# Four-layer graph network on one core: h of the last layer transposed by VectorE instead of TensorE, dot products and spreading of the scores moved

## The chip, the cores and the metric

The kernel runs on one core of one Trainium2 chip. The metric is the device time in microseconds (us) of one execution; lower is better. Three executions of the kernel before took 2621.48, 2621.51 and 2623.4 us (median 2621.51). Engines are named PE (TensorE matmuls), PEld (TensorE weight loads), DVE (VectorE), ACT (ScalarE), POOL (GpSimd) and SP (SyncE, which here only issues DMAs).

## The reference

64 graphs, each with x of 256 nodes by 512 features and an adjacency matrix adj of 256 by 256, all fp32. Four layers, each behind a layer norm and a relu, each added to x:

```
h = relu(layernorm(x));  x = x + layer(h)
layer 0: Wh = h W; e = leaky_relu(Wh a1 + (Wh a2)^T, 0.2), masked by adj > 0.5
         att = softmax(e, axis=1);  out = elu(att Wh)
layer 1: A1 = D^-1/2 (adj + I) D^-1/2;  out = relu(A1 h K + bias)
layer 2: out = relu((adj h) K), rows of h that are all zero masked
layer 3: out = relu([h, adj h / deg] W^T)
```

The output is x after the fourth layer, fp32. To keep fp32 accuracy, every matmul is done as three matmuls on a high and a low part of its operands (hi hi, hi lo, lo hi), in the fp32r type.

## The kernel before

**Staging.** Each pair (graph, layer) is a step k = 4 graph + 5 layer. So the layer of a step is k mod 4, and the steps of a layer follow each other at a distance of four. All engines run the same loop over slots j; in slot j each engine does its part of steps j-1 to j+5, so that five graphs are under way at once. A period is four slots and finishes one graph. Below, "slot 0" is every slot with j mod 4 = 0, and so on: in slot 0, step j is of layer 0, j+1 of layer 1, j+2 of layer 2, j+3 of layer 3. The order within a slot is written out by hand, engine by engine, and semaphores with counted values join the engines. An engine executes strictly in its order.

**A step of layers 0 to 2.** DVE takes the statistics of x (`statistics`, L540 to L545), POOL works out scale and bias (`normalise`, L730 to L741), ACT writes h (`activate`, L405) and its high part h_hi (`high_part`, L411), POOL the low part h_lo (`low_part`, L747). PE multiplies h by the adjacency matrix or the attention (`gather`, 24 matmuls of 256 columns) into the PSUM tile T; ACT and DVE split T into t_hi (`gathered`, L417) and t_lo (L595), in two halves each; PE multiplies by the weights (`project`, 24 matmuls of 512 columns) into O; in the next slot ACT, DVE and POOL apply the nonlinearity and add to x.

**Layer 3** has the order of products turned round, and needs h transposed. PE's `transpose_h` (L302 to L311) makes eight transposes of 128x128 blocks of h into the PSUM tile X; ACT copies them to ht_hi (L423), DVE makes ht_lo (L602). Then `project_first` (24 matmuls of 512 columns into T), `gathered`, and in `gather_last` 24 matmuls of 512 columns into X and 12 into O.

**Attention scores of layer 0.** `dots` (L554, DVE, four operations of 128x512) forms the products of h with two vectors; PE's `spread` (L298) transposes the result so that it lies along rows of X; DVE's `mask_scores` (L569 to L576), ACT's `exps` (L453, L457) and DVE's `softmax_parts` (L581 to L589) make the attention's parts p_hi and p_lo, which `gather` of layer 0 waits for.

**Order per slot in the kernel before** (what the step is of, in brackets):

- PE: slot 0 `gather`[1], `project`[0]; slot 1 `gather`[2], `transpose_h`[3], `project`[1]; slot 2 `spread`[0], `project_first`[3], `project`[2]; slot 3 `gather`[0], `gather_last`[3].
- DVE: slot 0 `mean_relu`[3] (L627, L630), `gathered`[1], `with_self` (L649 to L654, the adjacency with its diagonal for a later layer 1), `dots`[0]; slot 1 `positive_part`[0] (L608), `gathered`[2], `add_mask` (L562), `transposed`[3] (L602), `statistics`[1]; slot 2 `mask_scores`[0], `scaled_relu`[1] (L617, L620), `softmax_parts`[0], `gathered`[3], `statistics`[2]; slot 3 `degrees`, `gathered`[0], `without_self` (L661), `statistics`[3], `statistics`[0].
- ACT: slot 0 `activate`[3], `gathered`[1], `activate`[0], `with_self` (L465, then L467, which waits for DVE's a_diag of L649); slot 1 `elu`[0] (L436 twice, L439 twice), `gathered`[2], `high_part`[0], `transposed`[3] (L423); slot 2 `activate`[1], `exps`[0], first half of `gathered`[3], `high_part`[1], second half; slot 3 `masked_relu`[2], `gathered`[0], `activate`[2], `high_part`[2], `without_self`, `own_term`[3].
- POOL: slot 1 `elu`[0] (L712), `low_part`[0], `normalise`[1]; slot 2 `low_part`[1], `normalise`[2]; slot 3 `masked_relu`[2], `degrees`, `low_part`[2], `mask_rows`, `normalise`[3], `normalise`[0].
- SP: stores of out, loads of x, adj and adj_t, each behind the semaphore of the work that frees or fills its buffer.

T is one buffer: `t_free` (L289) makes PE wait for the t_lo of the step before, half by half. h, h_hi, h_lo, t_hi and t_lo have two buffers, by k mod 2; ht_hi and ht_lo have one. act_out[:, 1] holds the intermediate result of `scaled_relu` alone.

Of the kernel before, what the change touches and what calls it, by code (L numbers as in the profile page):

```python
# [5 lines left out]
F32 = mybir.dt.float32  # L6
# [3 lines left out]
AX = mybir.AxisListType  # L10

P = 128
LAYERS = 4
SPACING = 5
MASKED = -9000000000000000.0
# [55 lines left out]
def gnn_kernel(nc, x, adj, adj_t, w_all, a_vecs, bias, out):  # L71
# [8 lines left out]
    with ExitStack() as ctx:  # L80
        def sb(name, shape, dt=F32):
            return ctx.enter_context(nc.sbuf_tensor(name, shape, dt))

        def sem(name):
            return ctx.enter_context(nc.semaphore(name))

        w_hi = sb("w_hi", [P, WEIGHTS, FT, F], F32R)
        w_lo = sb("w_lo", [P, WEIGHTS, FT, F], F32R)
        distance = sb("distance", [P, 96])
# [51 lines left out]
        X = ctx.enter_context(nc.psum_tensor("X", [P, 2, F], F32))  # L141
        wh_rows = X[:, 0, 0:N]

        stage = [act_out[:, 0], act_out[:, 1], z[:], xs[:, 5], xs[:, 4], xs[:, 3], z[:], xs[:, 5], xs[:, 4], xs[:, 3]]
        halves_at = {-3: (0, 1), 0: (2, 3), 1: (4, 5), 2: (6, 7), 3: (8, 9)}

# [12 lines left out]
        ident_zero, ident_ready, minus_half_ready = sem("ident_zero"), sem("ident_ready"), sem("minus_half_ready")  # L159

        t_ready, o_ready = sem("t_ready"), sem("o_ready")
        wh_rows_ready, ht_psum_ready, z_psum_ready = sem("wh_rows_ready"), sem("ht_psum_ready"), sem("z_psum_ready")

        stats_ready, mv_ready, neg_mean_ready, var_ready, rstd_ready, scale_ready, ln_ready = (
            sem("stats_ready"), sem("mv_ready"), sem("neg_mean_ready"), sem("var_ready"), sem("rstd_ready"),
# [22 lines left out]
        def step(k):  # L188
            return Step(plan, k)

        def wait(eng, semaphore, value):
            if value > 0:
                eng.wait_ge(semaphore, value)

        def tiles(dram, g):
            return dram[g].rearrange("(m p) f -> p m f", p=P)

        def flat(t):
            return t.rearrange("p m n -> p (m n)")

        def flat_blocks(t):
            diag = t.rearrange("p m (b c) -> p (m b) c", b=NT)[:, 0:NT * NT:NT + 1]
# [69 lines left out]
        def _(pe):  # L272
# [18 lines left out]

            def spread(k):
                wait(pe, wh_ready, k.done(L0, DOTS))
                wait(pe, ht_lo_ready, k.done(L3, NT, back=1))
                wait(pe, scores_ready, k.done(L0, NT, back=4))
                wait(pe, z_ready, k.done(L3, NT, back=5))
                for m in range(NT):
                    last = nc.tensor.transpose(wh_rows[:, m * P:m * P + P],  # L298
                                               wh[:, k.g % 2, 0, m:m + 1].to_broadcast([P, P]), ident[:])
                last.then_inc(wh_rows_ready, 1)  # L300

            def transpose_h(k):  # L302
                wait(pe, h_ready, k.done(ALL, NT))
                wait(pe, z_ready, k.done(L3, NT, back=4))
                wait(pe, scores_ready, k.done(L0, NT, back=3))
                for half in range(2):
                    for f in range(HALF * half, HALF * half + HALF):
                        for m in range(NT):
                            c = (f % HALF) * N + m * P
                            last = nc.tensor.transpose(X[:, half, c:c + P], h[:, k.odd, m, f * P:f * P + P], ident[:])  # L310
                    last.then_inc(ht_psum_ready, 1)  # L311

            def gather(k):
                wait(pe, h_hi_ready, k.done(L012))
# [24 lines left out]
            def project_first(k):  # L339
                if k.g == 0:  # L340
                    wait(pe, w_lo_ready, 2 * WEIGHT_ORDER.index(4) + 2)
                wait(pe, ht_lo_ready, k.done(L3, NT))
                for n in range(NT):
                    t_free(k, n)
                    h_times(k, flat(T[:, HALF * n:HALF * n + HALF]), n, 4).then_inc(t_ready, 1)
# [29 lines left out]
                    product(O[:, k.odd, n], parts).then_inc(o_ready, 1)  # L375

            for j in slots:
                if step(j + 2).layer == 0:
                    spread(step(j + 2))
                if step(j + 1).layer in L012:  # L380
                    gather(step(j + 1))
                if step(j + 1).layer == 3:
                    project_first(step(j + 1))
                if step(j + 2).layer == 3:
                    transpose_h(step(j + 2))
                if step(j).layer in L012:
                    project(step(j))
                if step(j).layer == 3:
                    gather_last(step(j))

        @block.scalar
        def _(act):
# [5 lines left out]
            def activate(k):  # L398
                wait(act, ln_ready, k.done(ALL))
                wait(act, h_lo_ready, k.done(L012, NT, back=2))  # L400
                wait(act, wh_ready, k.done(L0, DOTS, back=2))
                wait(act, ht_psum_ready, k.done(L3, NT, back=2))
                for m in range(NT):
                    total = h_sum[:, k.ab, m:m + 1] if k.layer == 2 else None
                    nc.scalar.activation(h[:, k.odd, m], xs[:, k.xb, m], ACT.Relu, bias=ln_bias[:, k.quad, m:m + 1],  # L405
                                         scale=ln_scale[:, k.quad, m:m + 1], accum_out=total).then_inc(h_ready, 1)
# [11 lines left out]

            def transposed(k):
                wait(act, z_psum_ready, k.done(L3, NT, back=4))  # L420
                for half in range(2):
                    wait(act, ht_psum_ready, k.part(L3, NT, half))
                    nc.scalar.copy(ht_hi[:, HALF * half:HALF * half + HALF],  # L423
                                   X[:, half].rearrange("p (f n) -> p f n", f=HALF)).then_inc(ht_hi_ready, 1)

            def own_term(k):
                wait(act, out_ready, k.done(L3, back=4))
# [80 lines left out]
        def _(dve):  # L508
# [83 lines left out]
            def gathered(k, b):  # L592
                c = slice(HALF * b, HALF * b + HALF)
                wait(dve, t_hi_ready, k.part(ALL, NT, b))
                nc.vector.tensor_tensor(t_lo[:, k.odd, c], T[:, c], t_hi[:, k.odd, c].bitcast(F32),  # L595
                                        ALU.subtract).then_inc(t_lo_ready, 1)

            def transposed(k):
                for half in range(2):
                    c = slice(HALF * half, HALF * half + HALF)  # L600
                    wait(dve, ht_hi_ready, k.part(L3, NT, half))
                    nc.vector.tensor_tensor(ht_lo[:, c], X[:, half].rearrange("p (f n) -> p f n", f=HALF),  # L602
                                            ht_hi[:, c].bitcast(F32), ALU.subtract).then_inc(ht_lo_ready, 1)

            def positive_part(k):
                for n in range(NT):
# [4 lines left out]
            def scaled_relu(k):  # L611
                if k.g == 0:
                    dve.wait_ge(bias_in, 16)
                wait(dve, deg_rsqrt_ready, k.done(L0, back=SPACING))
                for n in range(NT):
                    wait(dve, o_ready, k.part(ALL, NT, n))
                    nc.vector.scalar_tensor_tensor(act_out[:, 1, n], O[:, k.odd, n], deg_rsqrt[:, k.xb, n:n + 1],  # L617
                                                   bias_rows[:], ALU.mult, ALU.add).then_inc(psum_taken, 1)
                wait(dve, psum_taken, k.done(L013, NT))
                nc.vector.scalar_tensor_tensor(flat(xs[:, k.xb]), flat(act_out[:, 1]), 0.0, flat(xs[:, k.xb]), ALU.max,  # L620
                                               ALU.add).then_inc(l1_done, 1)
# [42 lines left out]
            for j in slots:  # L664
                if j == -4:
                    weight_vectors()
                if step(j + 2).layer == 0:
                    mask_scores(step(j + 2))
                if step(j - 1).layer == 3:
                    mean_relu(step(j - 1))  # L670
                if step(j - 1).layer == 0:
                    positive_part(step(j - 1))
                if step(j - 1).layer == 1:
                    scaled_relu(step(j - 1))
                if step(j + 1).layer == 0:
                    degrees(step(j + 1))
                if step(j + 2).layer == 0:
                    softmax_parts(step(j + 2))
                if step(j + 1).layer is not None:
                    gathered(step(j + 1), 0)  # L680
                    gathered(step(j + 1), 1)
                if step(j + 5).layer == 1:
                    with_self(step(j + 5))
                if step(j + 4).layer == 0:
                    dots(step(j + 4))
                if step(j + 3).layer == 0:
                    add_mask(step(j + 3))
                if step(j + 2).layer == 3:
                    transposed(step(j + 2))
                if step(j + 3).layer == 2:  # L690
                    without_self(step(j + 3))
                if step(j + 4).layer in (1, 2, 3):
                    statistics(step(j + 4))
                if step(j + 5).layer == 0:
                    statistics(step(j + 5))
                for i in halves_at.get(j, ()):
                    split_weight(i)
# [96 lines left out]
```

## Time and profile before

| | |
|---|---|
| median of three runs | 2621.51 us |
| the profiled execution: its own time | 2621.74 us |
| its span, first to last instruction | 2619.9 us |
| PE busy | 2547.1 us (97%) |
| PEld busy | 2205.5 us (84%) |
| DVE busy | 1823.2 us (70%) |
| ACT busy | 1408.7 us (54%) |
| POOL busy | 1185.2 us (45%) |
| chain that ended last | PE 96%, each other engine 1% or less |
| TensorE's mean granted clock | 0.992 of full |
| DMA | 109.3 MB, mean 42 GB/s |

A row of the time order reads: start (us from the span's start), duration, engine, line, operation, output <- inputs with shapes, count, and in brackets how long the engine had been idle before and what released it. Operations of one engine overlap at their ends, so the distance from one start to the next can be shorter than a duration. Matmuls overlap still more: one of 512 columns lasts 0.39 us in the rows and the next starts 0.23 us later.

### The profile page before, as it was taken

The numbers are of one execution on the slowest core, as the hardware profiler recorded it, in microseconds if no ns is written. First come the engines' busy times: TensorE is split into PE (matmuls) and PEld (weight loads), VectorE is DVE, ScalarE is ACT, GpSimd is POOL, SyncE is SP. The second block draws the span as 40 slices with busy tenths as digits, with TensorE's granted clock in tenths as the row PEclk, the third lists the DMA queues.
The fourth block names the chain that finished last, engine by engine and source line by source line (L and its number), as shares of the span: only waits on it lengthen the run. The fifth ranks groups of instructions, "written<-read, shape, count | busy, mean of one in ns | idle before, by whom it ended". The sixth has DMA issues, their size and how long they took to land.

```text
span 2619.9 us, 40393 instructions
## 1 busy us (share of the span) xinstructions
PE 2547.1 (97%) x13704; PEld 2205.5 (84%) x13704; DVE 1823.2 (70%) x4251; ACT 1408.7 (54%) x2571; POOL 1185.2 (45%) x1607
## 2 busy tenths in 40 slices
PE   2799999999999999999999999999999999999998
PEld 2688888888888888888888888888888888888886
DVE  6776676676676677677677777777776766766753
ACT  3555555555555555555555555555555555555542
POOL 2544444444444444444444444444444444444431
PEclk8899999999999999999999999999999999999999
DMA  4101111111011011011111111111111111111000
GB/s 140 41 29 49 33 41 49 33 41 49 30 44 49 29 45 49 29 45 46 33 45 41 37 45 41 37 45 35 42 46 33 41 49 33 41 49 33 29 17 25
DMA packets 72844, 109.30 MB, mean 42 GB/s; under 512 B 4288, under 2 KB 37056, under 8 KB 72640
## 3 DMA queue, kind: packets, MB, share of 16 engines
q1 hardware_dynamic: 72640, 106.71, 12.6%
q8 instruction: 112, 1.84, 0.3%
q14 instruction: 92, 0.75, 0.1%
HBM read 73.14 MB, written 33.55 MB: 41 GB/s over the span
## 4 chain that ended last, share of the span: by engine, by line
PE 96%; DVE 1%; issue 1%; ACT 1%; POOL 1%; DMA 0%; SPq 0%; POOLq 0%; ACTq 0%; DVEq 0%
PE O L277 46%; PE T L277 34%; PE X L277 13%; PE X L310 2%; PE X L298 1%; POOL h_lo L747 0%; ACT h L405 0%; DMA act_out<-w_all 0%; POOL xs L712 0%; DVE p_lo L589 0%; DVE scores L522 0%; DVE w_lo L512 0%; DVE t_lo L595 0%; ACT act_out L436 0%; DVE xs L630 0%
## 5 line engine op out<-in xcount | busy, mean ns | idle before, releaser
L747 POOL TENSOR_TENSOR h_lo<-h,h_hi 128x512 fp32r<-128x512 f32 x384 | 503.4, 1333 | 673.1 <-ACT h_hi L411 673.1
L595 DVE TENSOR_TENSOR t_lo<-T,t_hi 128x512 fp32r<-128x512 f32 x512 | 352.5, 690 | 399.1 <-ACT t_hi L417 399.1
L405 ACT ACTIVATE h<-xs,ln_bias,ln_scale 128x512 f32<-128x512 f32 x512 | 396.0, 811 | 391.9 <-POOL ln_bias L741 391.9
L277 PE MATMUL O<-w_hi,t_hi 128*128 128x512 f32 x1536 | 603.2, 393 | 0.0
L277 PE MATMUL O<-w_hi,t_lo 128*128 128x512 f32 x1536 | 598.2, 389 | 0.0
L277 PE MATMUL O<-w_lo,t_hi 128*128 128x512 f32 x1536 | 598.1, 389 | 0.0
L417 ACT CAST t_hi<-T 128x512 fp32r<-128x512 f32 x512 | 298.3, 584 | 257.1 <-PE T L277 257.1
L712 POOL TENSOR_TENSOR xs<-xs,act_out 128x512 f32<-128x512 f32 x128 | 163.7, 1297 | 531.7 <-ACT act_out L439 496.9
L277 PEld LDWEIGHTS O<-w_hi,t_lo 128*128 128x128 f32 x1536 | 288.3, 188 | 60.2
L277 PEld LDWEIGHTS O<-w_hi,t_hi 128*128 128x128 f32 x1536 | 288.5, 188 | 55.9 <-DVE t_lo L595 0.5
L277 PEld LDWEIGHTS O<-w_lo,t_hi 128*128 128x128 f32 x1536 | 288.6, 188 | 55.7
L540 DVE BATCH_NORM_STATS2 ln_stats<-xs 128x6 f32<-128x512 f32 x512 | 326.7, 678 | 11.4 <-POOL xs L718 5.5
L277 PE MATMUL T<-a_hi,h_hi 128*128 128x256 f32 x1024 | 288.2, 281 | 3.0 <-DVE t_lo L595 3.0
L277 PE MATMUL T<-a_hi,h_lo 128*128 128x256 f32 x1024 | 287.8, 281 | 0.0
L277 PE MATMUL T<-a_lo,h_hi 128*128 128x256 f32 x1024 | 287.7, 281 | 0.0
L411 ACT CAST h_hi<-h 128x1024 fp32r<-128x1024 f32 x192 | 201.8, 1051 | 109.2 <-PE T L277 107.2
L277 PE MATMUL T<-w_hi,ht_hi 128*128 128x512 f32 x512 | 205.4, 401 | 4.2 <-DVE ht_lo L602 4.2
L277 PE MATMUL T<-w_lo,ht_hi 128*128 128x512 f32 x512 | 200.2, 391 | 0.0
L277 PEld LDWEIGHTS T<-a_hi,h_hi 128*128 128x128 f32 x1024 | 192.4, 188 | 9.1 <-issue 3.7
L277 PE MATMUL T<-w_hi,ht_lo 128*128 128x512 f32 x512 | 200.0, 391 | 0.0
L277 PE MATMUL X<-w_hi,ht_hi 128*128 128x512 f32 x512 | 199.2, 389 | 0.0
L277 PE MATMUL X<-w_lo,ht_hi 128*128 128x512 f32 x512 | 199.2, 389 | 0.0
(92 smaller groups left out, 4991.4 us busy)
## 6 DMA issues: line engine op xcount, KB each, us to landing
xs<-x SPq DMA_DIRECT2D x64, 512.0 KB, 3.6
out<-xs SPq DMA_DIRECT2D x64, 512.0 KB, 2.8
a_raw<-adj_t SPq DMA_DIRECT2D x64, 256.0 KB, 2.7
a_rows<-adj SPq DMA_DIRECT2D x64, 256.0 KB, 2.7
xs<-w_all SPq DMA_DIRECT2D x6, 512.0 KB, 7.3
act_out<-w_all SPq DMA_DIRECT2D x2, 512.0 KB, 6.7
z<-w_all SPq DMA_DIRECT2D x2, 512.0 KB, 6.4
v_rows<-a_vecs SPq DMA_DIRECT2D x1, 512.0 KB, 5.4
```

Source lines behind the costliest of these rows:

```text
L277: last = nc.tensor.matmul(psum, s, m, start=(start and n == 0 and i == 0), stop=(stop and n == len(pairs) - 1 and i == 2))
L298: last = nc.tensor.transpose(wh_rows[:, m * P:m * P + P], wh[:, k.g % 2, 0, m:m + 1].to_broadcast([P, P]), ident[:])
L310: last = nc.tensor.transpose(X[:, half, c:c + P], h[:, k.odd, m, f * P:f * P + P], ident[:])
L405: nc.scalar.activation(h[:, k.odd, m], xs[:, k.xb, m], ACT.Relu, bias=ln_bias[:, k.quad, m:m + 1], scale=ln_scale[:, k.quad, m:m + 1], acc ...
L411: nc.scalar.copy(h_hi[:, k.odd], h[:, k.odd]).then_inc(h_hi_ready, 1)
L417: nc.scalar.copy(t_hi[:, k.odd, c], T[:, c]).then_inc(t_hi_ready, 1)
L540: nc.vector.bn_stats(ln_stats[:, k.quad, m], xs[:, k.xb, m]).then_inc(stats_ready, 1)
L595: nc.vector.tensor_tensor(t_lo[:, k.odd, c], T[:, c], t_hi[:, k.odd, c].bitcast(F32), ALU.subtract).then_inc(t_lo_ready, 1)
L712: nc.gpsimd.tensor_tensor(xs[:, k.xb, n], xs[:, k.xb, n], act_out[:, 0, n], ALU.subtract).then_inc(pool_added, 1)
L747: nc.gpsimd.tensor_tensor(h_lo[:, k.odd, m], h[:, k.odd, m], h_hi[:, k.odd, m].bitcast(F32), ALU.subtract).then_inc(h_lo_ready, 1)
```

## The change

`transpose_h` on PE goes, and with it the PSUM tile X as its target. In its place VectorE moves 32x32 blocks: `turn` issues instructions of 32 partitions by 256 elements (eight blocks of 32x32 each), one for each pair of a source and a destination quarter of the partitions, 16 for a graph, into act_out[:, 1], which then holds the transposed h. Four of them stand in slot 0 ahead of `mean_relu`, twelve behind `gathered` and ahead of `with_self`. ACT's ht_hi and DVE's ht_lo are now one operation of 128x1024 each, read from SBUF instead of two of 128x512 from PSUM. `dots` moves from DVE's slot 0 to slot 1, behind `transposed`, with `add_mask` behind it; `spread` moves on PE from the head of slot 2 to behind `project_first`.

```
@@ tensor
             def spread(k):
                 wait(pe, wh_ready, k.done(L0, DOTS))
-                wait(pe, ht_lo_ready, k.done(L3, NT, back=1))
...
-            def transpose_h(k):
...
             def project_first(k):
...
-                wait(pe, ht_lo_ready, k.done(L3, NT))
+                wait(pe, ht_lo_ready, k.done(L3))
...
             for j in slots:
-                if step(j + 2).layer == 0:
-                    spread(step(j + 2))
                 if step(j + 1).layer in L012:
                     gather(step(j + 1))
                 if step(j + 1).layer == 3:
                     project_first(step(j + 1))
-                if step(j + 2).layer == 3:
-                    transpose_h(step(j + 2))
+                if step(j + 2).layer == 0:
+                    spread(step(j + 2))
@@ scalar
-                wait(act, ht_psum_ready, k.done(L3, NT, back=2))
+                wait(act, ht_ready, k.done(L3, TURNS, back=2))
...
             def transposed(k):
...
+                wait(act, ht_ready, k.done(L3, TURNS))
+                nc.scalar.copy(flat(ht_hi[:]), ht).then_inc(ht_hi_ready, 1)
@@ vector
+            def turn(k, blocks):
+                wait(dve, h_ready, k.done(ALL, NT))
+                wait(dve, l1_done, k.done(L1, back=3))
+                for n in blocks:
+                    i, o = divmod(n, QUADS)
+                    nc.vector.transpose(ht_blocks[QUAD * o:QUAD * o + QUAD, :, :, i],
+                                        h_blocks[QUAD * i:QUAD * i + QUAD, k.odd, :, :, o]).then_inc(ht_ready, 1)
...
             def transposed(k):
...
+                wait(dve, ht_hi_ready, k.done(L3))
+                nc.vector.tensor_tensor(flat(ht_lo[:]), ht, flat(ht_hi[:]).bitcast(F32),
+                                        ALU.subtract).then_inc(ht_lo_ready, 1)
...
             def scaled_relu(k):
+                wait(dve, ht_lo_ready, k.done(L3, back=-2))
...
                 if step(j + 2).layer == 0:
                     mask_scores(step(j + 2))
+                if step(j + 3).layer == 3:
+                    turn(step(j + 3), range(QUADS))
                 if step(j - 1).layer == 3:
                     mean_relu(step(j - 1))
...
                     gathered(step(j + 1), 1)
+                if step(j + 3).layer == 3:
+                    turn(step(j + 3), range(QUADS, TURNS))
                 if step(j + 5).layer == 1:
                     with_self(step(j + 5))
-                if step(j + 4).layer == 0:
-                    dots(step(j + 4))
-                if step(j + 3).layer == 0:
-                    add_mask(step(j + 3))
                 if step(j + 2).layer == 3:
                     transposed(step(j + 2))
+                if step(j + 3).layer == 0:
+                    dots(step(j + 3))
+                    add_mask(step(j + 3))
```

## Rows read from the trace of the kernel before

**Rows 1.** Busy time of each engine in one period of the steady stretch
```profile
1315.59:1355.15 39.56, 39.56 (x215) 34.31 (x214) 28.01 (x66) 21.84 (x41) 18.43 (x25) 1.00 0.13 41
```

**Rows 2.** TensorE in order of time: start us, us, engine, line, operation
```profile
1318.42 0.39 PE L277 MATMUL O<-w_hi,t_hi 128*128 128x512 f32 x1
...
1323.86 0.28 PE L277 MATMUL T<-a_hi,h_hi 128*128 128x256 f32 x1
...
1326.69 1.03 PE L310 MATMUL X<-ident,h 128*128 128x128 f32 x8
...
1333.03 0.38 PE L298 MATMUL X<-ident,wh 128*128 128x128 f32 x2
...
1338.70 0.39 PE L277 MATMUL O<-w_hi,t_hi 128*128 128x512 f32 x1
```

**Rows 3.** VectorE in order of time, slot 0
```profile
1315.66 1.41 DVE L627 SCALAR_TENSOR_TENSOR z<-O,deg_recip,z 128x512 f32<-128x512 f32 x2
...
1318.26 0.68 DVE L595 TENSOR_TENSOR t_lo<-T,t_hi 128x512 fp32r<-128x512 f32 x1
...
1319.24 0.69 DVE L595 TENSOR_TENSOR t_lo<-T,t_hi 128x512 fp32r<-128x512 f32 x1 [0.30 <-ACT t_hi L417]
...
1319.85 0.41 DVE L649 TENSOR_TENSOR a_diag<-a_raw,ident 128x256 f32<-128x256 f32 x1
```

**Rows 4.** ScalarE in order of time, slots 0 and 1
```profile
1315.36 1.52 ACT L405 ACTIVATE h<-xs,ln_bias,ln_scale 128x512 f32<-128x512 f32 x2 [1.73 <-POOL ln_bias L741]
...
1324.06 0.60 ACT L436 ACTIVATE act_out<-O 128x512 f32<-128x512 f32 x1 [2.06 <-PE O L277]
...
1324.55 1.14 ACT L439 ACTIVATE act_out<-act_out 128x512 f32<-128x512 f32 x2
...
1326.89 0.59 ACT L417 CAST t_hi<-T 128x512 fp32r<-128x512 f32 x1 [0.72 <-PE T L277]
...
1327.37 1.05 ACT L411 CAST h_hi<-h 128x1024 fp32r<-128x1024 f32 x1
```

**Rows 5.** Groups by line and form: busy us, mean ns, idle before
```profile
L654 DVE TENSOR_TENSOR a_lo<-a_diag,a_hi 128x256 fp32r<-128x256 f32 x64 | 26.8, 418 | 0.1
...
L585 DVE TENSOR_SCALAR p_hi<-scores,s_rec 128x256 fp32r<-128x256 f32 x128 | 39.4, 350 | 2.3
...
L620 DVE SCALAR_TENSOR_TENSOR xs<-act_out,xs 128x1024 f32<-128x1024 f32 x64 | 78.4, 1225 | 2.2
```

**Rows 6.** VectorE in order of time, slots 1 to 3
```profile
1330.15 1.27 DVE L540 BATCH_NORM_STATS2 ln_stats<-xs 128x6 f32<-128x512 f32 x2
...
1333.56 0.42 DVE L569 CUSTOM_DVE_ANT_0 scores<-X,mask_add 128x256 f32<-128x256 f32 x1 [1.71 <-PE X L298]
...
1337.24 0.16 DVE L581 RECIPROCAL s_rec<-s_sum 128x2 f32<-128x2 f32 x1
...
1338.76 0.68 DVE L595 TENSOR_TENSOR t_lo<-T,t_hi 128x512 fp32r<-128x512 f32 x1
...
1350.78 1.32 DVE L661 TENSOR_TENSOR a_lo<-a_raw,a_hi 128x256 fp32r<-128x256 f32 x1 [2.30 <-ACT a_hi L473]
```

**Rows 7.** ScalarE in order of time, slot 2
```profile
1333.39 1.52 ACT L405 ACTIVATE h<-xs,ln_bias,ln_scale 128x512 f32<-128x512 f32 x2 [3.99 <-POOL ln_bias L741]
...
1334.82 0.89 ACT L453 ACTIVATE scores<-scores,wh 128x256 f32<-128x256 f32 x2
...
1336.51 0.19 ACT L457 ACTIVATION_READ_ACCUMULATOR scores<-scores,s_neg 128x1 f32 x1
```

**Rows 8.** GpSimd in order of time, slot 3
```profile
1350.53 2.73 POOL L747 TENSOR_TENSOR h_lo<-h,h_hi 128x512 fp32r<-128x512 f32 x2 [3.37 <-ACT h_hi L411]
```

**Rows 9.** TensorE's idle time before a matmul, at both ends of the run
```profile
136.66 0.36 PE L277 MATMUL T<-a_hi,h_hi 128*128 128x256 f32 x1 [2.24 <-DVE t_lo L595]
...
2598.86 0.50 PE L277 MATMUL T<-w_hi,ht_hi 128*128 128x512 f32 x1 [2.50 <-DVE ht_lo L602]
```

**Rows 10.** Windows: length, busy and count of each engine, granted clock
```profile
2600.30:2603.70 3.40, 3.40 (x9) 2.66 (x9) 0.00 (x0) 0.52 (x1) 0.00 (x0) 0.50 0.02 5
```

More of the change, by code:

```diff
@@ L12 @@
 P = 128
+QUAD = 32
+QUADS = P // QUAD
+TURNS = QUADS * QUADS
 LAYERS = 4
@@ L85, in sem, with flat @@
             return ctx.enter_context(nc.semaphore(name))
+        def flat(t):
+            return t.rearrange("p m n -> p (m n)")
         w_hi = sb("w_hi", [P, WEIGHTS, FT, F], F32R)
@@ L142, in gnn_kernel @@
         wh_rows = X[:, 0, 0:N]
+        ht = flat(act_out[:, 1])
+        ht_blocks = ht.rearrange("p (c m q n) -> p m c q n", c=FT, m=NT, q=QUADS)
+        h_blocks = h[:].rearrange("p b m (c q f) -> p b m c q f", c=FT, q=QUADS)
         stage = [act_out[:, 0], act_out[:, 1], z[:], xs[:, 5], xs[:, 4], xs[:, 3], z[:], xs[:, 5], xs[:, 4], xs[:, 3]]
@@ L161, in gnn_kernel @@
         t_ready, o_ready = sem("t_ready"), sem("o_ready")
-        wh_rows_ready, ht_psum_ready, z_psum_ready = sem("wh_rows_ready"), sem("ht_psum_ready"), sem("z_psum_ready")
+        wh_rows_ready, ht_ready, z_psum_ready = sem("wh_rows_ready"), sem("ht_ready"), sem("z_psum_ready")
         stats_ready, mv_ready, neg_mean_ready, var_ready, rstd_ready, scale_ready, ln_ready = (
@@ L196, in tiles @@
             return dram[g].rearrange("(m p) f -> p m f", p=P)
-        def flat(t):
-            return t.rearrange("p m n -> p (m n)")
         def flat_blocks(t):
@@ L300, in spread @@
                 last.then_inc(wh_rows_ready, 1)
-            def transpose_h(k):
[L303 to L311, printed above, removed]
             def gather(k):
@@ L420, in transposed @@
                 wait(act, z_psum_ready, k.done(L3, NT, back=4))
[L421 to L424, printed above, removed]
+                wait(act, ht_ready, k.done(L3, TURNS))
+                nc.scalar.copy(flat(ht_hi[:]), ht).then_inc(ht_hi_ready, 1)
             def own_term(k):
@@ L596, in gathered @@
                                         ALU.subtract).then_inc(t_lo_ready, 1)
-            def transposed(k):
[L599 to L603, printed above, removed]
+            def turn(k, blocks):
[5 more added lines that the diff above has]
+                                        h_blocks[QUAD * i:QUAD * i + QUAD, k.odd, :, :, o]).then_inc(ht_ready, 1)
+            def transposed(k):
+                wait(dve, ht_hi_ready, k.done(L3))
+                nc.vector.tensor_tensor(flat(ht_lo[:]), ht, flat(ht_hi[:]).bitcast(F32),
+                                        ALU.subtract).then_inc(ht_lo_ready, 1)
             def positive_part(k):
```

## The prediction

> **What bounds the kernel now.** I read the windows by stage first. One period of the steady stretch, 39.56 us for one graph, has TensorE busy in all of it at the full granted clock, VectorE in 28.0 us, ScalarE in 21.8, GpSimd in 18.4 [rows 1]. So the time is the sum of TensorE's work, and each other engine has slack that matters only while it hides. Then TensorE's order of time: a `project` of 24 matmuls takes 5.44 us (1318.42 to 1323.86), a `gather` 2.83. The eight transposes begin at 1326.69 and the next `project` ends at 1333.03; less its 5.44 they cost 0.90 us. `spread` with the 5.44 of `project_first` takes 5.67, so 0.23 alone [rows 2]. Last I read the other engines' order of time around both places, for the start of each hand-over.
>
> Below, t is counted from the start of `gather`[1], at 1315.59 [rows 1]; TensorE now ends `project`[1] at 1333.03, which is t = 17.44, and without the transposes it would at 16.54.
>
> **What goes.** 0.90 us of the bounding engine in each graph. From TensorE's idle row at 136.66 to that at 2598.86 [rows 9] there are some 62 periods; I count 61. With all else hidden that is 55 us. ScalarE's two ht_hi of 128x512 become one of 128x1024, at the 1.05 us of h_hi [rows 4]; VectorE's two ht_lo become one at 1.23, the price of L620 with both inputs in SBUF [rows 5]. Neither total changes to speak of.
>
> **What is added: 16 moves on VectorE.** No row has a move of 32 partitions. By elements, 256, the nearest is L654 at 0.42 us [rows 5], whose like follow each other at 0.34 where nothing is between them (0.08 less than the duration, as the t_lo at 1319.24 with 0.69 is followed at 1319.85 [rows 3]). Lower bound 0.27, the spacing of the cheapest 256-element form (L585, 350 ns [rows 5]); upper bound 0.69, as though each of the 256 elements cost two. I take 0.42: I do not count on overlap between operations on different partitions, which no row shows. For 16 moves 6.7 us, for 0.34 5.4. VectorE's busy time becomes some 34.7 us of 38.7, so it does not become the bound by volume. It does by place.
>
> The Trainium skill speaks to this choice. Its page VectorE: DVE Perf Modes, section Two Vector instructions with no wait between them, says that an instruction whose source or destination starts in another quarter of the partitions than the last one's is held until all earlier VectorE work is finished. Here every move changes its destination quarter; by that rule there is no overlap, and the sum below stands, while without it the spacing would be 0.34 and the time that of the first variant under the ranges. No run here shows it yet.
>
> **Path A, to `project_first`.** Twelve of the moves stand ahead of `with_self`, and ScalarE's L467 waits there for a_diag; behind L467 in ScalarE's order are `elu`, `gathered`[2], `high_part`[0] and the ht_hi that TensorE's `project_first` needs. Step by step:
> - h of the last layer is there at 1316.88, t = 1.3 [rows 4]. Four moves: 3.0.
> - `mean_relu`, 2.60 from 1315.66 to 1318.26 [rows 3]: 5.6. It used to start at once; its store and the load of x behind it on SP go out 3 us later and have several slots of slack.
> - Two t_lo at the spacing of 0.61 [rows 3]: 6.8. Twelve moves, 5.0: 11.8.
> - a_diag 0.41 [rows 3]: 12.3; L467 on ScalarE, the same shape, 0.4: 12.7 (it used to start when a_diag came at 1319.85, t = 4.7).
> - `elu`: two at 0.49 and two in 1.04 [rows 4]: 14.7. Two t_hi at 0.48: 15.7. h_hi, 1.0: 16.7 [rows 4].
> - ht_hi 1.05: 17.7. ht_lo 1.23: 18.95.
> - GpSimd on top. The new ht_lo reads both inputs from SBUF, the old one read X. L661, 256 elements with both inputs in SBUF, begins at 1350.78 while GpSimd is in its first h_lo, and lasts 1.32 us against 0.42 for L654 [rows 5, 6, 8]. It ends about when that h_lo must have (1350.53 plus half of 2.73) plus its elements. So I let ht_lo wait for GpSimd's operation under way: `elu` there from 14.3, two of 1.3, first h_lo from 16.9 to 18.2, and ht_lo asks at 17.7. That adds 0.5: t = 19.5.
>
> TensorE is free at 16.54, so it idles 2.95 us.
>
> **Path B, to `gather`[0].** `spread` now follows `project_first`, with only `project`[2] between it and `gather`[0], which waits for p_lo and (T is one buffer) for the t_lo of `project_first`. In the trace, from `spread` at 1333.03 to that t_lo's end at 1339.44 is 6.41 us [rows 2, 6]; the cover is 5.67 [rows 2]. At least 0.75 us of idle. More, since slot 1 ends later. `spread` starts at 19.5 + 5.44 = 24.9. VectorE: `dots` wait for GpSimd's second h_lo until 20.8, then 0.5 and three of 0.61: 23.1; `add_mask` 0.4: 23.5. From the statistics at 1330.15 to `activate`[1] at 1333.39 is 3.24 [rows 6, 7]: 26.7. That is the time at which the scores' `exps` could start (24.9 plus 1.8, from 1333.03 to 1334.82), but `activate`[1] is ahead of them on ScalarE with 1.43: 28.2. `exps` until 1336.70 are 1.88 [rows 7]: 30.0. From s_rec at 1337.24 to the t_lo at 1338.76 1.52, and 0.68 for it [rows 6]: 32.3. `gather`[0] was due at 24.9 + 5.67 = 30.6: 1.7 us of idle.
>
> **The sum.** 39.56 - 0.90 + 2.95 + 1.7 = 43.3 us for a period, 3.75 more, times 61 is 229 us: 2621.7 (the profiled execution's own time, 1.8 over its span and within 0.3 of the median) + 229 = 2850.
>
> **The clock.** TensorE idle for 2.50 us at 2598.86 was followed by 3.4 us at half the clock (1.2 instead of 2.4 GHz); the idle 2.24 us at 136.66 was not followed by a fall [rows 9, 10]. An idle 2.95 us in every period may bring the fall in many. Each costs 1.7 us of TensorE's work; it delays `spread`, so path B shrinks to 0.8: 44.1 us, 4.55 more, 2899. I take half of the periods: **2875 us**.
>
> **Variants for the range.** Moves at 0.34: path A shorter by 1.3, its idle time 1.7, no fall of the clock: 2.5 more a period, 2774; with path B at its least 0.75, 2716. Moves at 0.27: idle 0.55 and 0.75 to 1.7, 0.4 to 1.35 more: 2646 to 2704. Moves at 0.50 with the clock's fall: 2978.
>
> **Rivals.**
> 1. *The moves hide.* Path A is covered if a move takes under 0.24 us (3.8 us less over 16 moves), below all rows of 256 elements. For it: nothing but that no row is of this kind. Even then path B leaves 0.75, so 0.15 less a period: 2612. Only with path B hidden too does the full 55 us come, 2566. The 0.75 stands on rows that the change does not touch. Faster 0.08, no change 0.03.
> 2. *The moves cost by 32x32 block,* 0.69 each: path A 4.3 longer, idle 7.3, with the clock's fall and path B at 0.75: 48.4 us, 3161. Chance 0.07.
> 3. *Path B alone:* moves at 0.27 or no wait for GpSimd, 2646 to 2704. Chance 0.1.
> 4. *The change does not take TensorE's transposes off:* ruled out, the diff deletes them and nothing else uses L310.
>
> The forecast, both paths visible with moves of 0.34 to 0.50, gets 0.72. A difference under 0.2% (5 us) could not be told from none. Faster and no change (0.11) and rival 2 (0.07) lie outside the range 2660 to 2980, which takes in most of rival 3. Faster 0.08, same 0.03, slower 0.89.
>
> **What would show it.** Right: TensorE idle some 3 us before each `project_first`, put down to ht_lo, and about 1 to 2 us before each `gather`[0], put down to t_lo; ScalarE idle before L467 by some 7 us; `elu` at t = 12.7 instead of 5.8; ht_lo over 1.5 us for GpSimd's sake; a move's spacing of 0.42; windows with the clock under 1.00 in the steady stretch. Wrong: TensorE without idle time (rival 1), a move of another duration (rival 2 or the variants), ht_lo at 1.23 (no conflict with GpSimd), or an idle time before `project`[1], which I have left out.

## The result, and the profile after

The changed kernel takes 3053.24 us (median of four runs, 3047.48 to 3065.38) against 2621.49 us: a ratio of 1.1652, 95% interval 1.1612 to 1.1693. It is slower, as forecast, but by 432 us where 253 were forecast, and outside the range of 2660 to 2980. The span of the profiled execution is 3056.4 us, its time 3058.17.

From the page of the changed kernel: busy time, the granted clock in 40 slices, and the chain that ended last.

```profile
PE 2644.8 (87%) x13192; PEld 2235.0 (73%) x13192; DVE 2401.6 (79%) x5211; ACT 1378.0 (45%) x2507; POOL 1253.7 (41%) x1607
...
PEclk8899999999999999999999999999999999999998
...
DVE 41%; PE 21%; ACT 19%; issue 15%; POOL 3%; ACTq 0%; DMA 0%; POOLq 0%; DVEq 0%; SPq 0%
```

TensorE's share of the chain has fallen from 96% to 21%: the chain now runs through VectorE and ScalarE and crosses to TensorE where it waits. The clock row reads 9 in most slices and hides what matters here, since a 9 holds for 0.94 as for 0.99. Windows show it: two periods, and a stretch inside the second (length, busy time and count of PE, PEld, DVE, ACT, POOL, granted clock, DMA share, GB/s).

```profile
1300.90:1344.90 44.00, 39.13 (x207) 33.17 (x207) 36.43 (x82) 21.24 (x40) 19.32 (x25) 1.00 0.12 36
1344.90:1391.90 47.00, 41.72 (x208) 35.06 (x207) 37.33 (x82) 21.31 (x40) 19.64 (x25) 0.93 0.11 34
1360.50:1367.20 6.70, 5.42 (x13) 4.26 (x14) 6.63 (x15) 0.00 (x0) 2.36 (x2) 0.50 0.00 0
```

They answer to the one window of before [rows 1]. The first period ran at the full clock and took 44.0 us; the second had 6.7 us at half the clock (1.2 GHz) and took 47.0. The groups that carry the change, then TensorE's idle times around them (L595 is the move, L600 ht_lo, L458 the cast that waits for a_diag, which was L467 before, L580 p_lo):

```profile
L595 DVE STREAM_TRANSPOSE act_out<-h 32x256 f32<-32x256 f32 x1024 | 446.8, 436 | 112.6 <-ACT h L398 82.4
...
L600 DVE TENSOR_TENSOR ht_lo<-act_out,ht_hi 128x1024 fp32r<-128x1024 f32 x64 | 99.7, 1558 | 66.5 <-ACT ht_hi L415 66.3
...
L458 ACT CAST a_hi<-a_diag 128x256 fp32r<-128x256 f32 x64 | 26.0, 407 | 476.5 <-DVE a_diag L648 476.5
...
L580 DVE SCALAR_TENSOR_TENSOR p_lo<-scores,s_rec,p_hi 128x256 fp32r<-128x256 f32 x128 | 100.8, 829 | 0.0
```

```profile
1317.76 0.50 PE L284 MATMUL T<-w_hi,ht_hi 128*128 128x512 f32 x1 [3.39 <-DVE ht_lo L600]
...
1330.67 0.36 PE L284 MATMUL T<-p_hi,h_hi 128*128 128x256 f32 x1 [1.48 <-DVE t_lo L586]
...
1361.78 0.79 PE L284 MATMUL T<-w_hi,ht_hi 128*128 128x512 f32 x1 [3.40 <-DVE ht_lo L600]
...
1377.61 0.36 PE L284 MATMUL T<-p_hi,h_hi 128*128 128x256 f32 x1 [1.88 <-DVE t_lo L586]
```

Both idle times are where the working put them, and close to its sizes: 3.4 us before `project_first` (2.95 forecast), 1.5 to 1.9 before `gather`[0] (1.7 or 0.8 forecast). A move takes 0.436 us. ScalarE waits 476.5 us in all, 7.8 a period, for a_diag. What is new is the time at half the clock: 1361.78 lies in it, and the matmul there lasts 0.79 us. VectorE's twelve moves, then p_lo in the first and in the second period, and GpSimd's h_lo in the second:

```profile
1304.74 5.58 DVE L595 STREAM_TRANSPOSE act_out<-h 32x256 f32<-32x256 f32 x12
...
1328.94 0.88 DVE L580 SCALAR_TENSOR_TENSOR p_lo<-scores,s_rec,p_hi 128x256 fp32r<-128x256 f32 x2
...
1374.86 1.89 DVE L580 SCALAR_TENSOR_TENSOR p_lo<-scores,s_rec,p_hi 128x256 fp32r<-128x256 f32 x2
```

```profile
1375.02 2.87 POOL L749 TENSOR_TENSOR h_lo<-h,h_hi 128x512 fp32r<-128x512 f32 x2 [6.18 <-ACT h_hi L404]
```

In the second period the pair of p_lo takes twice as long, with h_lo beginning between the two; b2 and b3 below take this apart.

### The profile page after: what moved, and what is told of

The parts are those of the page before. It is cut to its first block, busy times and chain, and to the rows that moved or that the text cites. A ratio compares the mean times of both kernels' runs of the same rounds, so it can differ in the third digit from the quotient of the medians.

```text
span 3056.4 us, 40270 instructions
## 1 busy us (share of the span) xinstructions
PE 2644.8 (87%) x13192; PEld 2235.0 (73%) x13192; DVE 2401.6 (79%) x5211; ACT 1378.0 (45%) x2507; POOL 1253.7 (41%) x1607
## 4 chain that ended last, share of the span: by engine, by line
DVE 41%; PE 21%; ACT 19%; issue 15%; POOL 3%; ACTq 0%; DMA 0%; POOLq 0%; DVEq 0%; SPq 0%
PE T L284 19%; DVE act_out L595 13%; ACT h L398 7%; DVE t_lo L586 4%; DVE ln_stats L531 3%; ACT h_hi L404 3%; DVE z L626 3%; DVE p_lo L580 3%; DVE a_lo L660 3%; DVE ht_lo L600 2%; ACT t_hi L410 2%; ACT act_out L427 2%; ACT ht_hi L415 2%; DVE act_out L616 2%; POOL ln_scale L735 2%
## 5 line engine op out<-in xcount | busy, mean ns | idle before, releaser
L749 POOL TENSOR_TENSOR h_lo<-h,h_hi 128x512 fp32r<-128x512 f32 x384 | 573.4, 1514 | 394.5 <-ACT h_hi L404 392.4
L595 DVE STREAM_TRANSPOSE act_out<-h 32x256 f32<-32x256 f32 x1024 | 446.8, 436 | 112.6 <-ACT h L398 82.4
L284 PE MATMUL T<-w_hi,ht_hi 128*128 128x512 f32 x512 | 248.1, 485 | 228.5 <-DVE ht_lo L600 228.5
L586 DVE TENSOR_TENSOR t_lo<-T,t_hi 128x512 fp32r<-128x512 f32 x512 | 334.0, 682 | 111.2 <-ACT t_hi L410 109.2
L284 PEld LDWEIGHTS T<-w_hi,ht_hi 128*128 128x128 f32 x512 | 119.4, 233 | 281.6 <-DVE ht_lo L600 251.0
L284 PE MATMUL T<-p_hi,h_hi 128*128 128x256 f32 x512 | 163.3, 319 | 135.6 <-DVE t_lo L586 106.7
L458 ACT CAST a_hi<-a_diag 128x256 fp32r<-128x256 f32 x64 | 26.0, 407 | 476.5 <-DVE a_diag L648 476.5
L284 PE MATMUL T<-w_lo,ht_hi 128*128 128x512 f32 x512 | 236.1, 461 | 0.0
L284 PE MATMUL T<-w_hi,ht_lo 128*128 128x512 f32 x512 | 233.6, 456 | 0.0
```

What stands on the lines that cost most here:

```text
L284: last = nc.tensor.matmul(psum, s, m, start=(start and n == 0 and i == 0), stop=(stop and n == len(pairs) - 1 and i == 2))
L595: nc.vector.transpose(ht_blocks[QUAD * o:QUAD * o + QUAD, :, :, i], h_blocks[QUAD * i:QUAD * i + QUAD, k.odd, :, :, o]).then_inc(ht_ready, 1)
L749: nc.gpsimd.tensor_tensor(h_lo[:, k.odd, m], h[:, k.odd, m], h_hi[:, k.odd, m].bitcast(F32), ALU.subtract).then_inc(h_lo_ready, 1)
```

## The experiments

Ten further kernels were run: four made from the changed kernel (a1, a3, a4, a5), two from the kernel before (b2, b3), and c1, a reordering of the changed one, with three made from it (c2 to c4). Periods given as a mean are measured over 58 periods, from the first matmul of one `gather`[0] to that of the next; before it is 39.57 us, in the changed kernel 46.27.

**a1: a_diag ahead of the twelve moves.**

```
                     gathered(step(j + 1), 1)
-                if step(j + 3).layer == 3:
-                    turn(step(j + 3), range(QUADS, TURNS))
                 if step(j + 5).layer == 1:
                     with_self(step(j + 5))
+                if step(j + 3).layer == 3:
+                    turn(step(j + 3), range(QUADS, TURNS))
```

> The changed kernel with VectorE's with_self ahead of the second twelve moves, nothing else. Theory (order: L458 on ScalarE waits for a_diag, and elu, gathered, high_part and ht_hi queue behind it; plus the idle time before gather[0]; plus falls of the clock): ScalarE's 7.8 us of waiting before L458 go, path A becomes VectorE's own: moves end at t = 13.9, positive_part 15.1, two t_lo 16.3, ht_lo behind GpSimd's operation 18.3, so TensorE idles about 1.8 us before project_first instead of 3.4; before gather[0] it idles some 2.4, since dots start late relative to spread. Period some 42.9 us, 2820, and up to 2900 with falls of the clock. Rival (volume: VectorE's 7.5 us more per graph set the time, wherever they stand): 3050, as the changed kernel.

Measured: 2944.99 us, ratio 1.1234 [1.1217, 1.1251], 108 us less than the changed kernel. ScalarE's wait for a_diag fell from 476.5 to 125.8 us, TensorE's idle time before `project_first` to 1.7, that before `gather`[0] rose to 2.6; the mean period is 44.44. The two idle times came near what the theory had (1.8 and 2.4), the total did not: it is 45 us over the upper end. The shortest periods, without a fall of the clock, take 43.4 us where 42.9 were expected; with 43.4 in all 58 the total would be near 2885 (2945 less 58 times 1.0). So the falls cost some 60 us here (the clock is 0.97 in 700 to 1300 us), within the 80 that the expectation allowed for them; too low were the period without a fall, by 0.5 us, and the ends of the run, which it counted as ordinary periods. The place of a_diag is a real part of the loss, and volume alone is out.

**a3: half of the moves.** TURNS is 8 instead of 16; the other half of the transposed h is left out.

> The changed kernel with 8 moves instead of 16 (four and four): it leaves out half of the transposed h. Theory (order and clock): path A is 8 x 0.468 = 3.7 us shorter, its idle time (3.4) gone; the idle time before gather[0] stays, at 0.8 to 1.7; no falls of the clock in the steady stretch. Period 39.4 to 40.4, so 2615 to 2680, about 2650. Rival (volume): half of the loss stays, 2840. Rival (the falls of the clock come from the idle time before gather[0], or from anything but path A): falls go on, over 2700.

Measured: 2694.23 us, ratio 1.0274 [1.0257, 1.0291]. From the steady stretch, 700 to 1300 us (columns as above), and TensorE's waits over the whole run:

```profile
700.00:1300.00 600.00, 577.77 (x3067) 494.09 (x3066) 492.00 (x1092) 314.73 (x577) 285.10 (x371) 1.00 0.12 40
```

```profile
PE T L284 <- DVE t_lo L586: 96.9, 63, 3.8
...
PE T L284 <- DVE ht_lo L600: 15.5, 2, 8.2
```

The idle time before `project_first` is gone but for two times at the end, that before `gather`[0] stays at 1.5 us, and the clock is 1.00. VectorE still makes eight moves, 3.7 us, per graph, and 73 us of the loss are left where the rival (volume) had half of it. The mean period is 40.39, which is 38.7 (the period without any idle time, from c1 below) plus 1.5 plus 0.2: an idle time costs a little more than its length. It is counted from the end of the matmul before it, which lasts 0.39 us where the next one would have started 0.23 us after its start, so 0.16 us of overlap is lost with it; and the first matmul after it is slower (0.50 us instead of 0.39 for the one at 1317.76 above). The total is 14 us above the expected range. 58 periods explain 48 of the 73 us; the rest lies at the ends of the run.

**a4: scores where they were.** In the changed kernel, `dots` back in slot 0 behind `with_self`, `add_mask` ahead of `transposed`, `spread` at the head of slot 2.

> The changed kernel with dots, add_mask and spread where they were before the change: dots in slot 0 behind with_self, spread at the head of slot 2. Theory: the idle time before gather[0] goes (cover 11 us again); path A stays, and dots stand in it now, so TensorE's idle time ahead of project_first or spread is 3.5 to 4.5; falls of the clock behind it go on. Period 42.5 without falls, 44 to 45 with them: 2880 to 2960. Rival (the moved scores cause most of the loss): idle time and falls go, below 2750. Rival (volume): 3050.

Measured: 3041.14 us, ratio 1.16 [1.1583, 1.1617]. No idle time before `gather`[0]; before `project_first` it is 5.2 us in every period, more than the 3.5 to 4.5 expected, and the clock in 700 to 1300 us is 0.94. Mean period 46.08. The total is 81 us over the upper end of what was expected, and so near the 3050 of the rival (volume) that this run can't tell the two apart; a1, with the same moves and 108 us less, and c1 do that. What it does show: the moved scores are not what makes the change slow. Without their move the time is the same, since the `dots` then stand in path A.

**b2: the moved scores alone.** The kernel before with the change's order of `dots`, `add_mask` and `spread`; the transposes stay on TensorE.

```
-                if step(j + 2).layer == 0:
-                    spread(step(j + 2))
...
                 if step(j + 1).layer == 3:
                     project_first(step(j + 1))
+                if step(j + 2).layer == 0:
+                    spread(step(j + 2))
...
-                if step(j + 4).layer == 0:
-                    dots(step(j + 4))
-                if step(j + 3).layer == 0:
-                    add_mask(step(j + 3))
                 if step(j + 2).layer == 3:
                     transposed(step(j + 2))
+                if step(j + 3).layer == 0:
+                    dots(step(j + 3))
+                    add_mask(step(j + 3))
```

> The kernel before with only dots, add_mask and spread moved as in the change; transposes stay on TensorE. Theory (path B by itself): chain from spread to the t_lo of project_first 6.4 us against a cover of 5.7, TensorE idle 0.75 us before each gather[0] as long as activate[1] is not ahead of the exps, up to 1.5 if it is; no falls of the clock. 2665 to 2715. Rival (path B costs nothing by itself, it shows only where slot 1 ends late): 2621.

Measured: 2783.07 us, ratio 1.062 [1.0604, 1.0636], far above the expected 2665 to 2715. Path B costs more by itself than its chain: VectorE and GpSimd in the order of time, then TensorE's idle time and the window behind it.

```profile
1340.94 1.90 DVE L589 SCALAR_TENSOR_TENSOR p_lo<-scores,s_rec,p_hi 128x256 fp32r<-128x256 f32 x2
```

```profile
1341.13 2.84 POOL L746 TENSOR_TENSOR h_lo<-h,h_hi 128x512 fp32r<-128x512 f32 x2 [6.57 <-ACT h_hi L411]
```

```profile
1300.48 0.36 PE L277 MATMUL T<-p_hi,h_hi 128*128 128x256 f32 x1 [1.85 <-DVE t_lo L595]
```

```profile
1301.60:1304.80 3.20, 3.20 (x17) 3.20 (x17) 2.35 (x9) 0.58 (x1) 2.32 (x5) 0.50 0.17 37
```

The pair of p_lo takes 1.90 us instead of 0.88: GpSimd's h_lo of layer 1 begins at 1341.13, between the two. h_hi of layer 1 used to wait for TensorE's `project_first` (107 us in all in the kernel before); with `spread` behind `project_first` that wait is over long before, and h_hi and h_lo come early, into the softmax. The idle time is 1.85 us, not 0.75, and even behind 1.85 us the clock falls, in some of the periods (21 falls in the 58; mean 42.21 us, 41.6 where it does not fall).

**b3: b2 with the conflict taken out.** One wait more: GpSimd's h_lo of layer 1 behind p_lo.

```
             def low_part(k):
...
+                if k.layer == 1:
+                    wait(pool, p_lo_ready, k.done(L0, NT, back=1))
```

> The run b2 (the kernel before with only dots, add_mask and spread moved) with one wait more: GpSimd's h_lo of layer 1 starts when p_lo is finished. Theory (in b2 the second p_lo, with two inputs in SBUF, waits for GpSimd's h_lo, 1.90 us for the pair instead of 0.88, because h_hi of layer 1 no longer has project_first to wait for): p_lo's pair back to 0.88, the idle time before gather[0] from 1.85 to 0.8, no falls of the clock; 2675 to 2700 instead of 2783. Rival (p_lo is long for another reason): p_lo's pair stays at 1.9, 2783.

Measured: 2687.83 us, ratio 1.0249 [1.0234, 1.0264], 95 us less than b2 by a wait that was added. VectorE, GpSimd, and the steady window:

```profile
1338.68 0.88 DVE L589 SCALAR_TENSOR_TENSOR p_lo<-scores,s_rec,p_hi 128x256 fp32r<-128x256 f32 x2
```

```profile
1339.73 2.53 POOL L748 TENSOR_TENSOR h_lo<-h,h_hi 128x512 fp32r<-128x512 f32 x2 [7.43 <-DVE p_lo L589]
```

```profile
700.00:1300.00 600.00, 587.46 (x3159) 504.96 (x3159) 425.39 (x973) 319.10 (x590) 267.54 (x365) 1.00 0.12 40
```

p_lo's pair is back at 0.88, the idle time at 0.83, no fall of the clock: the bare path B, as worked out in the prediction (0.75). The Trainium skill has the rule for the conflict, in its page SBUF — State Buffer, section SBUF: two separate sides: a VectorE operation with two SBUF inputs and a GpSimd operation that reads SBUF exclude each other for the whole instruction. b2 and b3 agree with it: the lock, and not the work, made 1.0 us.

**a5: TensorE kept busy.** Twelve matmuls into X, which is free then, ahead of the wait for ht_lo.

```
             def project_first(k):
...
+                wait(pe, z_ready, k.done(L3, NT, back=4))
+                for i in range(12):
+                    nc.tensor.matmul(X[:, 1], w_hi[:, 0, i % FT, 0:P], w_lo[:, 0, i % FT], start=True, stop=True)
                 wait(pe, ht_lo_ready, k.done(L3))
```

> The changed kernel with twelve matmuls of 512 columns (2.7 us) on TensorE ahead of project_first's wait; they write X, which nothing reads before it is written again, so the result stays. Theory (a large part of the loss is the clock's: TensorE's idle time of 3.4 us is followed by 3.4 or 6.8 us at half the clock): the other engines' paths stay, the idle time before project_first shrinks to 0.7 us, that before gather[0] stays at 1.5 to 1.9; few or no falls of the clock, periods 44.0 to 44.3 instead of 46.4, 2900 to 2930 (with a few falls behind gather[0]'s idle time up to 2960). Rival (the clock's falls sit in time in which TensorE would wait anyway, so they cost nothing): 3050. Rival (more work on TensorE is more time): 3050 to 3200.

Measured: 2930.97 us, ratio 1.118 [1.1161, 1.1198], 1 us over the expected range: 122 us less, by 2.7 us more work for TensorE in each graph. ScalarE's wait for a_diag is the same as in the changed kernel, and the clock is full:

```profile
ACT a_hi L461 <- DVE a_diag L651: 476.8, 61, 9.2
```

```profile
700.00:1300.00 600.00, 570.98 (x2974) 483.85 (x2973) 494.56 (x1094) 290.58 (x532) 263.32 (x341) 1.00 0.12 38
```

The idle times are 0.73 and 1.49 us, the mean period 44.13, and no period is longer than 44.4. The few periods of the changed kernel without a fall take the same, 44.0 to 44.1. This is the run that gives the clock its price: 46.27 - 44.13 = 2.1 us a period, 122 us in all. Some 0.3 of the 2.1 are the longer idle time before `gather`[0] (1.78 us on the mean in the steady stretch of the changed kernel), which comes with the falls.

**c1: the moves in an order in which they hide.** From the changed kernel, on TensorE and VectorE:

```
                 for n in range(NT):
+                    if n == 1 and step(k.k + 1).layer == 0:
+                        spread(step(k.k + 1))
...
-                if step(j + 3).layer == 3:
-                    turn(step(j + 3), range(QUADS))
                 if step(j - 1).layer == 3:
                     mean_relu(step(j - 1))
+                if step(j + 3).layer == 3:
+                    turn(step(j + 3), range(QUADS))
...
                 if step(j + 3).layer == 3:
                     turn(step(j + 3), range(QUADS, TURNS))
-                if step(j + 5).layer == 1:
-                    with_self(step(j + 5))
+                if step(j + 3).layer == 1:
+                    add_self(step(j + 3))
+                if step(j + 2).layer == 1:
+                    with_self(step(j + 2))
```

So `mean_relu` is ahead of the first four moves, `with_self` is out of slot 0, and `spread` stands between the two halves of `project_first`. `add_self` is the first operation of `with_self` (a_diag) by itself, in slot 2; the rest of `with_self` is in slot 3. On ScalarE `with_self` follows `masked_relu` in slot 3; in slot 2 `exps` and `gathered`(0) come ahead of `activate`[1], and `high_part`[1] behind `gathered`(1); in slot 1 `transposed` is ahead of `high_part`[0]. On GpSimd, in slot 1, `low_part`[0] follows `normalise`[1].

> The changed kernel in another order: mean_relu ahead of the first four moves; with_self taken out of slot 0 (a_diag at the end of VectorE's slot 2, the rest in slot 3, ScalarE's two casts there ahead of gathered); spread between the two halves of project_first; ScalarE's exps ahead of activate[1] and ht_hi ahead of h_hi in slot 1; GpSimd's h_lo of layer 0 behind normalise[1]. Theory (order, not volume): VectorE's path to ht_lo ends at t = 15.9, ahead of TensorE's 16.5; the path from spread has a cover of 8.4 us against 6.4 to 6.8. No idle time on TensorE but traces, no falls of the clock, period 38.7 to 39.2: 2570 to 2600, below the kernel before. Rival (volume: VectorE at 92% of a period of 38.7 us can't be ordered so that nothing waits): idle times of 1 us or more remain somewhere, 2650 or more.

Measured: 2597.48 us, ratio 0.9905 [0.9891, 0.992]: below the kernel before. One period of it, and TensorE's longest waits over the whole run:

```profile
1296.00:1334.70 38.70, 38.70 (x207) 33.27 (x206) 37.64 (x81) 21.46 (x40) 19.67 (x26) 1.00 0.13 42
```

```profile
PE T L284 <- DVE ht_lo L604: 21.1, 2, 11.9
PE T L284 <- DVE p_lo L584: 18.9, 2, 10.1
```

VectorE is busy in 37.6 of 38.7 us (its waits for GpSimd are part of that) and TensorE never waits in it. So the volume of the moves fits, with the period 0.85 us shorter than before, the 0.90 of the transposes nearly whole. Of the gain of 49 us in 58 periods half is lost at the ends: TensorE waits twice for ht_lo there, 21.1 us together, as in the last graphs nothing hides the moves. The total is at the upper end of what was expected for that reason. c1 moves several things at once; c3 and c4 take back one each, and what the others are worth by themselves was not tried.

**c2: both ways of transposing.** c1 with TensorE's transposes for the first two and the last two graphs.

```
+        def by_vector(g):
+            return 2 <= g < G - 2
...
+                if step(j + 2).layer == 3 and not by_vector(step(j + 2).g):
+                    transpose_h(step(j + 2))
```

> c1 with TensorE's transposes (as before the change) for the first two and the last two graphs, where TensorE idles anyway, and VectorE's moves for the 60 between. Theory (c1's steady stretch has the full gain, 38.7 us a period; it loses some 25 us at both ends, where nothing hides the 7.5 us of moves: TensorE waits 9.2 and 11.9 us for ht_lo at the end, with falls of the clock behind): the end becomes as short as before, 2575 to 2585. Rival (the ends are longer because of the other order, not of the moves): 2597.

Measured: 2582.04 us, ratio 0.9852 [0.9837, 0.9866]: the fastest, 39 us under the kernel before. The wait for ht_lo at the end is down to two of 2.4 us:

```profile
PE T L297 <- DVE ht_lo L633: 4.9, 2, 2.4
```

**c3: c1 with `spread` behind `project_first`,** as in the change.

> c1 with spread behind project_first, as in the change, nothing else. Theory (path B: chain of 6.4 us or more from spread to the t_lo of project_first against a cover of 5.7): idle time before gather[0] of 0.8 to 1.2 us in each period, no falls of the clock; 2645 to 2675. Rival (with exps ahead of activate[1] the chain is short enough): 2597.

Measured: 2763.34 us, ratio 1.054 [1.0523, 1.0558], 88 us over the expected range. The idle time before `gather`[0] is back, 1.35 to 2.2 us and not the 0.8 to 1.2 expected, with falls of the clock behind it (0.99 in 700 to 1300 us), so the place of one pair of transposes of 0.23 us makes 166 us. Part of the surplus is again the lock, on the smallest of operations:

```profile
1322.32 0.76 DVE L566 SCALAR_TENSOR_TENSOR s_neg_max<-s_max,wh 128x2 f32<-128x2 f32 x1
```

```profile
1320.52 2.54 POOL L756 TENSOR_TENSOR h_lo<-h,h_hi 128x512 fp32r<-128x512 f32 x2
```

s_neg_max works on two elements per partition and takes 0.76 us instead of 0.16: it begins at 1322.32, in the second of the two h_lo, and ends at 1323.08, as that h_lo ends (1320.52 plus 2.54 is 1323.06).

**c4: c1 with h_lo of layer 0 ahead of `normalise`[1],** as in the change.

> c1 with GpSimd's h_lo of layer 0 ahead of normalise[1] again, as in the change, nothing else. Theory (an operation of VectorE with two inputs in SBUF and one of GpSimd exclude each other, one whole operation at a time): ht_lo and dots wait for h_lo, up to 1.3 us each, dots end 2 to 2.6 us later and TensorE waits 1 to 2 us for them ahead of spread; 2650 to 2720. Rival (they share without loss, or VectorE has slack for it): 2597.

Measured: 2709.0 us, ratio 1.0334 [1.0318, 1.0349]. VectorE's `dots`, GpSimd, and TensorE's idle time before `spread`:

```profile
1328.31 1.77 DVE L549 CUSTOM_DVE_ANT_0 scores<-h,v_rows 128x512 f32<-128x512 f32 x1
...
1330.02 1.76 DVE L549 CUSTOM_DVE_ANT_0 mask_add<-h,v_rows 128x512 f32<-128x512 f32 x1
```

```profile
1327.25 3.99 POOL L758 TENSOR_TENSOR h_lo<-h,h_hi 128x512 fp32r<-128x512 f32 x2
```

```profile
1333.07 0.43 PE L304 MATMUL X<-ident,wh 128*128 128x128 f32 x2 [1.62 <-DVE wh L549]
```

Two of the four `dots` take 1.77 us instead of 0.68, and TensorE waits 1.6 us a period, within the expected range. ht_lo did not get longer, as the theory had it: it takes 2.02 us here and 2.01 in the steady stretch of c1. The change costs 112 us, from nothing but the time at which GpSimd does the same work. The clock stays full behind these 1.6 us.

## Why the prediction was wrong in size, step by step

- **What bounds before, and what goes:** right. 0.90 us a graph; c1's period of 38.72 against 39.57 shows 0.85 of it.
- **The move at 0.42 us:** short. It lasts 0.436 and the next one starts 0.468 us after the last (5.58 us for twelve, less the last one's 0.436, over eleven): there is no overlap, even a gap of 0.03. The rule of the Trainium skill that the prediction weighs (VectorE: DVE Perf Modes, Two Vector instructions with no wait between them: held while the quarter changes) agrees with this row; the overlap of 0.08 that other operations of 128 partitions show is absent. 16 times 0.048 is 0.8 us a period.
- **Path A:** right in its members: four moves, `mean_relu`, twelve moves, a_diag, L458, `elu` and on to ht_lo, which waits for GpSimd (1.56 us instead of 1.23, 1.7 forecast). Idle time 3.39 against 2.95, the surplus from the moves. a1 and a3 show it by its parts.
- **Path B:** right in place, 1.48 us in periods at the full clock against 1.7. But the prediction has it shrink to 0.8 when the clock falls; it is 1.88 then. `spread` comes later, the p_lo pair then meets GpSimd's h_lo, and b2 and b3 show that this costs 1.0 us; without it some 0.9 would be left, as the prediction had it. The prediction had seen the lock for ht_lo and `dots` and not looked for it at p_lo.
- **The period without falls of the clock:** 43.3 forecast, 44.1 measured (a5). This part of the working alone would have given 2850 us; with the measured period over 58 periods, 0.8 more each, it is 48 us higher. The two idle times are 0.2 us longer together than forecast (3.39 and 1.48 against 2.95 and 1.7). The rest, some 0.6, is mostly what an idle time costs over its length, 0.2 us and more for each of the two (a3), for which the prediction has no term.
- **The clock is the step that failed.** The prediction has it: "Each costs 1.7 us of TensorE's work; it delays `spread`, so path B shrinks to 0.8: 44.1 us, 4.55 more, 2899. I take half of the periods". That is 0.4 us a period on the mean. It cost 2.1. In the 47.0 us period above the half clock lasted 6.7 us, not 3.4, path B did not shrink, and few periods are free of it: the mean over 58 is 46.27 where those without a fall take 44.1. Three things were mis-sized. One fall of 3.4 us in the kernel before was taken as the size of all falls, half of the periods as their number, and none was foreseen at `gather`[0]. The record of the granted clock in the trace has 55 falls in the 58 periods, 24 of 6.8 us and 31 of 3.4, and 17 of the 55 are at `gather`[0]. That is 4.6 us at half the clock a period, where the forecast has 1.7. Over 58 periods the difference is some 99 us.
- **The ends of the run:** the prediction counts them as periods like the others. a5 against before is 309 us, of which 58 periods at 4.56 are 265; 45 lie at the ends, 34 more than three periods of 3.75. c1 and c2 show what they are: moves of 7.5 us which nothing hides.

The three surpluses, 48, 99 and 34 us, make 181; the miss is 3053 - 2875 = 178.

The rivals: that the moves hide was refuted for this order (a move of 0.436 where 0.24 was needed), and so was a price of 0.69. (Rival 1 says 3.8 us less over 16 moves; 3.8 is the length of 16 such moves, and the saving needed is the 2.95.) That VectorE's volume is no bound was right, and c1 shows it with 37.6 of 38.7 us busy. Why one idle time brings 3.4 us at half the clock, another 6.8 and a third none was not tried by itself and stays open.

## What to carry to other kernels

Work taken off the bounding engine pays only if the engine that takes it over has room at that place in its order: here a gain of 0.9 us a period became a loss of 6.7, and the same moves in another order gave the gain. Look first at what stands behind the added work in its engine's queue and who waits for that (here the operand of a later layer, a_diag, held up ScalarE and so everything); then at which pairs of VectorE and GpSimd operations now meet. And when a walk through the orders shows TensorE idle for a microsecond or two in every period, as here, the clock's fall must be priced as a term of its own, taken from several falls and not from one; as a test of it, matmuls that do nothing useful, put into the idle time, are cheap.

## What the runs showed of the hardware that was not expected

- Idle times of 1.85 us (b2) and 3.4 us a period were followed by half clock in the same kernel in some periods and not in others; of 1.48, 1.6 and 0.83 (a3, c4, b3) in none of the steady stretch. In the kernel before, 2.24 was not followed by a fall and 2.50 was [rows 9, 10]. In the changed kernel's steady stretch no wait of 1.5 us before `gather`[0] had a fall; of the waits of 1.9 us, all in periods with a fall before them, about two in five had another.
- 2.7 us of useless matmuls in each graph made the changed kernel 122 us faster.
- A VectorE operation of 128x2 elements can take 0.76 us instead of 0.16 for a GpSimd operation under way (c3), and ht_lo of c1 takes 1.97 on the mean instead of the 1.23 of an operation of its size (L620 before); both count as VectorE's busy time, so that a busy share of 97% can hold waits.
- A move of 32 partitions by 256 fp32 elements takes 0.436 us, and in the changed kernel the next one always starts at least 0.03 us after it has ended.
